# Centring the first chunk only, rotating it tile by tile out of PSUM, and loading late what is needed late

## The reference, cut to what matters

```python
x = x + attn(_layernorm(x), ...)      # no gamma, no beta
x = x + ffn(_layernorm(x), ...)
# in attn:
q = (x @ Wq.T).reshape(B, S, H, hd).transpose(0, 2, 1, 3)   # k, v alike
q = layernorm(q, q_gamma, q_beta)     # over the 8 entries of a head, eps 1e-5
q = q * cos + rotate_half(q) * sin    # k alike
scores = scale * jnp.einsum('bhqd,bhkd->bhqk', q, k)        # causal, softmax, times v, @ Wo.T + bo
```

## Time and profile before

| | us |
|---|---|
| median of 3 runs (lowest, highest) | 383.33 (382.54, 387.38) |
| the profiled execution, its own time | 383.55 |
| its span, first to last instruction | 381.7 |
| PE busy | 338.2 (89%) |
| DVE busy | 291.7 (76%) |
| ACT busy | 233.5 (61%) |
| POOL busy | 181.1 (47%) |

### The profile page before, as it was taken

One profiled execution on the slowest core, in us unless ns is written; L12 is line 12 of the kernel. 1 busy time (PEld: TensorE's weight loads), 2 busy tenths in 40 slices (PEclk: granted clock), 3 DMA queues, 4 the chain that ended last, 5 costly groups with the idle time before them and its releaser, 6 DMA issues.

```text
span 381.7 us, 7937 instructions
## 1 busy us (share of the span) xinstructions
PE 338.2 (89%) x2883; PEld 148.3 (39%) x2883; DVE 291.7 (76%) x508; ACT 233.5 (61%) x340; POOL 181.1 (47%) x304
## 2 busy tenths in 40 slices
PE   2667689899799898999999989999999999969995
PEld 1233345445444334353334332434334433434342
DVE  5693789899999999779998899987686830656742
ACT  1656129776759566774576767786676999424320
POOL 1587985998855438657504502034060028471000
PEclk9966559999999999999999999999999999988999
DMA  4997004103200036002043130001000019000000
GB/s 124 200 217 162 16 3 127 43 3 92 78 3 4 0 106 149 2 0 72 0 100 87 38 75 2 3 1 30 2 2 2 3 53 202 0 0 0 3 27 27
DMA packets 26840, 19.65 MB, mean 51 GB/s; under 512 B 9713, under 2 KB 23570, under 8 KB 26738
## 3 DMA queue, kind: packets, MB, share of 16 engines
q1 hardware_dynamic: 25410, 18.09, 20.8%
q10 hardware_dynamic: 1392, 1.05, 1.2%
HBM read 11.56 MB, written 1.15 MB: 33 GB/s over the span
## 4 chain that ended last, share of the span: by engine, by line
PE 61%; DVE 24%; issue 5%; ACT 5%; DMA 2%; POOL 1%; ACTq 1%; SPq 1%; DVEq 0%; POOLq 0%
PE psum L766 14%; PE psum L718 13%; PE psum L782 7%; PE psum L695 7%; PE psum L672 7%; DVE mx_diag L1159 7%; PE psum L644 5%; DVE mx_full L1159 4%; ACT probs L842 2%; PE psum L626 2%; DVE mv L1249 2%; PE psum L635 1%; PE psum L736 1%; PE psum L728 1%; DVE resid L1148 1%
## 5 line engine op out<-in xcount | busy, mean ns | idle before, releaser
L842 ACT ACTIVATE probs<-psum 128x1024 f32<-128x1024 f32 x144 | 142.3, 1024 | 49.7 <-PE psum L644 27.1
L1159 DVE TENSOR_REDUCE mx_diag<-psum 128x4 f32<-128x512 f32 (+2 forms) x96 | 96.0, 1041 | 23.3 <-PE psum L672 22.6
L1159 DVE TENSOR_REDUCE mx_full<-psum 128x2 f32<-128x1024 f32 x64 | 76.1, 1220 | 7.3 <-PE psum L672 7.0
L718 PE MATMUL psum<-probs,v_ones 128*18 128x512 f32 (+3 forms) x768 | 73.6, 489 | 0.2
L766 PE MATMUL psum<-x2T,w 128*128 128x512 f32 x144 | 71.8, 626 | 1.0 <-DVE mv L1249 0.9
L672 PE MATMUL psum<-k_st,q_st 62*128 62x512 bf16 (+3 forms) x384 | 60.6, 344 | 2.0 <-ACT probs L842 0.9
L644 PE MATMUL psum<-masks 64*128 64x128 bf16 (+2 forms) x896 | 51.5, 216 | 11.0 <-DVE mx_diag L1159 3.3
L695 PE MATMUL psum<-q_st,k_st 64*128 64x512 bf16 (+3 forms) x384 | 53.7, 328 | 3.1 <-DVE mv L1249 0.9
L644 PEld LDWEIGHTS psum<-masks 64*128 64x128 bf16 x896 | 33.6, 96 | 42.8 <-DVE mx_diag L1159 14.9
L1077 POOL TENSOR_SCALAR mh<-mh 128x512 f32<-128x512 f32 x27 | 16.8, 623 | 62.3 <-ACT mh L895 62.1
L1084 POOL TENSOR_TENSOR mh<-mh,mv 128x512 f32<-128x512 f32 x27 | 34.1, 1270 | 11.8 <-DVE mv L1249 11.8
(11 more groups left out here) (162 smaller groups left out, 359.0 us busy)
## 6 DMA issues: line engine op xcount, KB each, us to landing
early<-combine_scratch SPq DMA_DIRECT2D x24, 256.0 KB, 4.8
q_st<-parts SPq DMA_DIRECT2D x24, 128.0 KB, 2.4
k_st<-parts SPq DMA_DIRECT2D x18, 128.0 KB, 2.4
w<-in_We SPq DMA_DIRECT2D x3, 512.0 KB
k_st<-in_c_pad SPq DMA_DIRECT2D x8, 128.0 KB, 6.3
out<-xs SPq DMA_DIRECT2D x4, 256.0 KB, 2.3
xs<-in_x SPq DMA_DIRECT2D x3, 256.0 KB, 5.9
k_st<-parts ACTq DMA_DIRECT2D x6, 128.0 KB, 4.0
```

The source lines that it names most:

```text
L718: last = pe.matmul(acc[32 * j:32 * j + 2 * VC, q0:q0 + cols], own_then_zeros, probs[:, n % P_RING, j % 2, col:col + cols], start=(kt == 0 ...
L842: act.activation(probs[:, n % P_RING, :, :], wpair("scores", (s, i)), ACT.Exp, scale=SCALE).then_inc(exp_done, 1)
L1159: dve.tensor_reduce(dst[:, a % 2, :, pairs[0]:pairs[0] + nm, qt], w, AX.X, ALU.max, negate=True).then_inc(max_free, 1)
```

## The change

- For chunk 0, `norm` is now `centre` on DVE: a sum over the features and one operation that subtracts the mean. `stats` (means, variances and the factor on the heads' epsilon, `eps_x`) follows behind it, and POOL works out the deviation (`norm_rstd.0`) for v alone.
- Chunk 0's `qkv` becomes four `qk` products of 256 columns and one stage `vx` with the four v products. ACT only squares q and k (`square`) and copies v with the scale (`v_read`).
- `rotate` on DVE, once for each tile, multiplies q and k by cosine and sine straight from PSUM, adds the two products and sums the squares. The heads' deviation comes after that and is multiplied in by `scaled_and_shifted`, first for q (`rope_q`, which alone releases `qT.0`), then for k (`rope`).
- The rotary table and the four small vectors are issued by ACT behind x instead of by SP.
- `rest_loads` (8 pads of the stacks, Wo, the router's weights, bo) become the stage `late.0`, in SP's queue behind chunk 0's stacks; `expert_loads` (15 DMAs) become `late.1`, between `mrow.2` and `mrow.3`.
- The whole of `ORDER` is another sequence. Of what the prediction speaks of: ACT has `norm_apply.1` and `v_read.0` between `square.2` and `square.3`; on POOL `norm_rstd.2` now stands between `kT_low.0` and `rstd_pool.1`, and `tables_pool.0` between `kT_low.1` and `mneg.3`; chunk 2's `norm_apply`, `xT` and `qkv` come behind the first maxima. Behind the last attention product (`pv.79`) PE had six expert products ahead of `proj.3` and has three.

```diff
-NORM_ON_DVE = (("norm", 0), ("norm2", NX - 1))
+NORM_ON_DVE = (("norm2", NX - 1),)
+weights.0@0 ones.0 ones.1 norm.0 stats.0 weights_read.0 tables.0 xT.0@4 xT_read.0 qk.0@3 qk.1@6 square.0 norm.1 square.1
+vx.0@4 qk.2@5 square.2 norm_rstd.0 norm_rstd.1 norm_apply.1 rotate.0 v_read.0 rotate.1 qk.3@1 square.3 xT.1@6 xT_read.1
+qkv.4@4 qkv.5@2 qkv.6@0 rotate.2 rotate.3 qkv_read.4 qkv_read.5 qkv_read.6 qkv.7@2 qkv_read.7 headrstd.0 rope_q.0 rope.0
+qT.0@6 qT_lead.0 qT_rest.0 qT_mid.0 norm.2 qT_low.0 stack.0.0.0 kT.0@2 kT_lead.0 kT_rest.0 stack_act.0.1.0 norm.3
...
-            sp.dma_start(rope[:, :, :, :], c_rope).then_inc(ld_rope, 16)
-            for n, v in enumerate((q_gamma, q_beta, k_gamma, k_beta)):
-                sp.dma_start(gb[:, n, :], v.partition_broadcast(P)).then_inc(ld_rope, 16)
+                if kind == "late":
+                    (rest_loads, expert_loads)[arg]()
...
+            def first_qk(t):
+                w = fill("qk", t)
+                pe.wait_ge(work_read_act, frees("act", max(FILL["weights", 0], FILL["xT", 0]) + 1))
+                pe.matmul(w[:, 0:2 * P], xnT[:, t * P:(t + 1) * P], w_qkv[:, 0:2 * P], start=True, stop=True
+                          ).then_inc(work_full, 1)
+
+            def first_v():
+                w = fill("vx", 0)
+                pe.wait_ge(work_read_act, frees("act", max(FILL["weights", 0], FILL["xT", 0]) + 1))
+                for t in range(TPC):
+                    last = pe.matmul(w[:, t * P:(t + 1) * P], xnT[:, t * P:(t + 1) * P], w_qkv[:, 2 * P:3 * P],
+                                     start=True, stop=True)
+                last.then_inc(work_full, 1)
...
+            act.dma_start(rope[:, :, :, :], c_rope).then_inc(ld_rope, 16)
+            for n, v in enumerate((q_gamma, q_beta, k_gamma, k_beta)):
+                act.dma_start(gb[:, n, :], v.partition_broadcast(P)).then_inc(ld_rope, 16)
...
+            def first_squares(t):
+                act.wait_ge(work_full, turned("qk", t))
+                both = wbank("qk", t)[:, 0:2 * P].rearrange("p (n d m) -> p n d m", n=4, d=HD)
+                act.activation(sq[0][:, t, :, :, :, :].rearrange("p w r m d -> p (w r) d m"), both, ACT.Square
+                               ).then_inc(squared, 1)
+
+            def first_values():
+                act.wait_ge(work_full, turned("vx", 0))
+                act.wait_ge(norm_ready, 1)
+                act.wait_ge(v_set, 1)
+                for t in range(TPC):
+                    last = act.activation(v_ones[:, 0, t, 0:H, 1, 0:HD],
+                                          wbank("vx", 0)[:, t * P:(t + 1) * P].rearrange("p (h d) -> p h d", h=H),
+                                          ACT.Identity, scale=rstd[:, 0, 0, t:t + 1])
+                last.then_inc(work_read_act, 1)
...
+                    if step == 2 and kind == "norm" and x == 0:
+                        last.then_inc(norm_ready, 1)
+                        return
...
+            def centre():
+                link(dve.tensor_reduce(sums_x[:, :], xs[:, 0, :, :], AX.X, ALU.add))
+                dve.scalar_tensor_tensor(out=xn[0], in0=sums_x[:, :].unsqueeze(2).broadcast_to([P, TPC, P]), scalar=-1.0 / P,
+                                         in1=xs[:, 0, :, :], op0=ALU.mult, op1=ALU.add).then_inc(xn_ready, 1)
+
+            def first_stats():
+                for t in range(TPC):
+                    last = dve.bn_stats(stats[:, 0, 0, t, :], xs[:, 0, t, :])
+                link(last)
+                for t in range(TPC):
+                    last = dve.bn_aggr(mean_var[:, 0, 0, t, :], stats[:, 0, 0, t, :])
+                link(last)
+                dve.tensor_scalar(eps_x[:, :], mean_var[:, 0, 0, :, 1], EPS, EPS, ALU.add, ALU.mult).then_inc(norm_stats, 1)
+
+            def rotate(t):
+                dve.wait_ge(squared, t + 1)
+                z = wbank("qk", t)[:, 0:2 * P]
+                by_head = z.rearrange("p (n d m) -> p n d m", n=4, d=HD)
+                cos = g_cos[:, 0, t, :, :, :].rearrange("p w k d -> p (w k d)").unsqueeze(2).broadcast_to([P, 4 * HD, H // 2])
+                sin = g_sin[:, 0, t, :, :, :].rearrange("p w k d -> p (w k) d")
+                own = qk[0][:, t, :, :, :, :].rearrange("p w k d m -> p (w k d) m")
+                other = roped[:, t, :, :, :, :].rearrange("p w k d m -> p (w k) d m")
+                dve.tensor_tensor(own, z.rearrange("p (n m) -> p n m", m=H // 2), cos, ALU.mult)
+                for j in range(2):
+                    last = dve.tensor_tensor(other[:, :, 4 * j:4 * j + 4, :], by_head[:, :, 1 - j::2, :],
+                                             sin[:, :, 4 * j:4 * j + 4].unsqueeze(3).broadcast_to([P, 4, 4, H // 2]), ALU.mult)
+                link(last)
+                dve.tensor_tensor(own, own, roped[:, t, :, :, :, :].rearrange("p w k d m -> p (w k d) m"), ALU.add)
+                dve.tensor_reduce(ssum[:, 0, 2 * H * t:2 * H * (t + 1)], sq[0][:, t, :, :, :, :].rearrange("p w k m d -> p (w k m) d"),
+                                  AX.X, ALU.add).then_inc(work_read_dve, 1)
+
+            def scaled_and_shifted(w):
+                z = qk[0][:, :, w, :, :, :]
+                by_head = hrstd[:, :].rearrange("p (t w k m) -> p t w k m", t=TPC, w=2, k=2)[:, :, w, :, :]
+                for k in range(2):
+                    last = dve.tensor_tensor(z[:, :, k, :, :], z[:, :, k, :, :],
+                                             by_head[:, :, k, :].unsqueeze(2).broadcast_to([P, TPC, HD, H // 2]), ALU.mult)
+                link(last)
+                added = g_add[:, 0, :, w, :, :].rearrange("p t k d -> p t (k d)").unsqueeze(3).broadcast_to([P, TPC, 2 * HD, H // 2])
+                return dve.tensor_tensor(roped[:, :, w, :, :, :].rearrange("p t k d m -> p t (k d) m"),
+                                         z.rearrange("p t k d m -> p t (k d) m"), added, ALU.add)
...
+                sums = ssum[:, 0, :].rearrange("p (t n) -> p t n", t=TPC)
+                link(dve.scalar_tensor_tensor(out=sums, in0=sums, scalar=1.0 / HD, in1=eps_x[:, :].unsqueeze(2).broadcast_to(
+                    [P, TPC, 2 * H]), op0=ALU.mult, op1=ALU.add))
```

## The result

The changed kernel takes 392.73 us (median of 4 runs, 391.83 to 394.89), the kernel before 383.94 on the same chips: a ratio of 1.0281, interval 1.0223 to 1.0338. Forecast were 381.0 us and a range of 375.5 to 386.5; the result lies above it. The profiled execution took 394.89 us, with a span of 393.1.

The account below looks back on a forecast made before the run. The prediction took PE, busy 89% of the span, as the fullest engine, idle mainly in the first 60 us. Gains of 1.1 + 1.5 - 0.5 + 0 + 0, plus 0.4 for the clock, gave 383.55 - 2.5 = 381.05 us, range 375.5 to 386.5.

Parts of the forecast that it names:

- Step 1: Prologue up to the rotation: centring readies xnT near 8.2 us, first square at 9.8; gain so far 2.4 us.
- Step 2: Chunk 0's rotation on DVE: 1.5 us per tile, three through at 15.2; the fourth, behind norm_apply.1, ends at 21.5.
- Step 3: From the heads' sums to the first maxima: hrstd at 25.0, first maxima at 37.5 (36 to 39), 2.5 us gained.
- Step 4: Chunk 1's stacks and maxima: stacks land at 68.1 instead of 69.2, gaining 1.1 us, plus 1.5 of earlier PE work.
- The rival of the half clock: Chunk 2's transposes and products among first maxima at half clock: up to 3 us lost, 384 to 385; chance 0.07.
- Step 5: Late expert loads on SP ahead of mrow.3: scores.9 waits nothing to 5 us, taken as half a microsecond.
- Step 6: Middle and end: reordered stages worth minus 4 to plus 4 us, value 0; fewer expert products before proj.3, value 0.
- The sum: Whole kernel: 1.1 + 1.5 - 0.5 + 0 + 0 = 2.1, plus 0.4 for an earlier full clock: 2.5 us faster.
- The tell-tales: Signs of failure: scores.9 waiting microseconds for a DMA, middle waits changing by over 4, first maxima at 40 again.

Follow-up runs that it names:

- e3: Changed kernel with the rotary table and four gamma/beta loads back on SP behind the centring matrix: 392.91 us, ratio 1.0252 to the kernel before.
- e8: Changed kernel with routing stages apart, pads after chunk 0's stacks land, expert loads in five groups of three: 393.43 us, ratio 1.0249 to the kernel before.
- e7: New arithmetic, order of the kernel before from the first maxima on, loads up front, chunk 2's products between first maxima: 385.84 us, ratio 1.0074 to the kernel before.
- e16: Like the hybrid of new arithmetic and old order, loads up front, but chunk 2's products ahead of the first maxima: 381.50 us, ratio 0.9960 to the kernel before.
- e17: Kernel before with only the 15 expert loads late, in one block behind mrow.2: 390.30 us, ratio 1.0214 to the kernel before.
- e2: Changed kernel with both groups of late loads before SP's first stack: 389.91 us, ratio 1.0172 to the kernel before.
- e15: Kernel before with chunk 0's routing stages 2 and 3 directly behind stage 1 on DVE: 387.97 us, ratio 1.0163 to the kernel before.
- e11: New arithmetic, old order, chunk 2's products ahead of first maxima, pads after chunk 0's stacks, expert loads in pieces: 382.27 us, ratio 1.0010 to the kernel before.
- e14: New arithmetic, old order, chunk 2's products before first maxima, late loads in pieces, mturn.0 later, centring loads and square.3 first: 379.10 us, ratio 0.9920 to the kernel before.
- e4: Kernel before with both load groups late: pads behind mneg.0, expert loads behind mrow.2: 390.41 us, ratio 1.0203 to the kernel before.

## Why the prediction was wrong

- **Step 1** failed in one sentence: "The loads that move to ACT's queue cost nothing". ACT's issues are free, their data aren't: issued beside x and the weights they hold back the matrix, which lands at 7.85 and, with them back on SP behind it, at 5.23 (e3). Given the early matrix, the working holds: e3's `xnT` is done at 8.13 (forecast 8.2) and its first square starts at 9.45 (9.8).
- **Step 2** was right in mechanism and size: `rotate` takes 1.6 us (1.5), `square.3` ran behind `norm_apply.1` at 19.09, the fourth rotation ended at 21.35 (21.5). The third one ended at 17.76 and not at 15.2, by the error of step 1; the end came out right because POOL's second chain sets it, as forecast, and that chain doesn't need the matrix.
- **Step 3** holds to the issues: `hrstd` at 24.95 (25.0), q at 26.5 and k at 27.9 (26.5, 28.0), ACT's last DMA at 33.54 (33.8). The term behind is mis-sized: that DMA took 5.82 us, not 2.4 to 3.7, and the first maxima came at 40.25 instead of 37.5, outside my ends of 36 to 39. About 1.5 us of it are the pads (e8), which is what I had let them count for, so the rest of the miss, 2.8 us on DVE, is there without them (e8: 38.76 where the sum had 36). That the stacks' own transfers make it up is likely and not shown.
- **Step 4** failed: chunk 1's maxima came at 72.22 instead of 68.1. POOL's rotation ended at 58.2 (57), and "4 us of that were slack" didn't hold: `qT.1` came at 60.16, 3.3 us behind the earlier trace rows. Two things then arrive together. Chunk 0's 24 reductions ended near 71.7 instead of 68.7, with chunk 2's products and `pv.1`, `pv.2` between them. And the stacks landed at 72.2: the low parts were done at 65.6, near the forecast 64.7, but SP's twelve issues, begun at 61.47, take 0.6 us each, and the last started at 69.71, not at 65.6. The sum had no term for that queue. The `pv` products I counted among "1.5 us of PE work done earlier", a gain; chunk 2's products stood in it only as 0.4 us gained by an earlier full clock, and e7 against e16 shows them as a loss of 3 to 4 us. The rival of the half clock had this mechanism, at up to 3 us and a chance of 0.07.
- **Step 5** failed in what it took. I had the bounds (7 to 13.2 us of issues, 0 to 5 us of stall) and the waiting stage right, and took about 8.5 us of issues and half a microsecond, because "the queues are nearly empty there". The issues took 12.8 us and the stall was 1.83; the DMA engines were 0.76 busy meanwhile, with the block's own data among them. The shared experts' weights, 64 KB each, take 1.9 us to issue where the large ones take 0.4. The nearest row was the 13.2 us, the only measurement there was. e17 prices the block at 2.1% in the kernel before, e2 both groups at 1.1% here.
- **Step 6** failed as much: "value 0" for an order of 1326 stages. The new order costs about 4 us (e7 against e2), at the end of my bounds. One cause is shown in the old order, the row of routing (e15); it was in the list that I read. I compared counts of stages ahead of chosen marks and never asked how long DVE does nothing that PE waits for.
- **The sum** was minus 2.5; it should have been about plus 10, as the chain of runs adds up: 1.1% for the loads (changed kernel to e2), 1.0% for the order (e2 to e7), 1.1% for chunk 2's products (e7 to e16), less the 0.4% that e16 leaves for the prologue, an interval that holds zero. Each link is uncertain by 0.5 to 0.8 of a per cent.
- **The tell-tales** that I named did show it: `scores.9` waiting 1.83 us for a DMA, waits in the middle changed by 5, first maxima at 40 again.

## What to carry to other kernels

A load taken out of the prologue isn't free where it goes: count its issue time on the queue, name the first small DMA behind it and who waits for that, and split the block or put it where the queue is idle. In a hand-written order, look for the longest row of one engine's work that the bounding engine doesn't need; moving the stage that shows the wait only hands the wait on. Before speeding up what comes first, find what sets the next hand-over: here chunk 1's rotation on POOL, so that 2.75 us (e11) and 4.1 us (e14) won at the first maxima were worth 0.6 and 0.3 us at 69 us.

## What the runs showed of the hardware

- DVE's operations on 128x64 elements with two SBUF inputs take 0.22 us as a rule, and 1.57 and 2.39 us in the routing of the changed kernel, while POOL made operations of 1.97 and 2.35 us on 128x1024; each of the two ends 0.08 us behind the POOL operation beside it. The two make the row of routing 3.5 us longer. That isn't new, though: the kernel before has five such operations in its routing, 3.3 us in all, but not in one row. The Trainium skill (SBUF — State Buffer, Who interferes with whom) has DVE and GpSimd lock their shared port for a whole instruction; the trace agrees, with an eleven-fold time here.
- In `late.1` of the changed kernel an issue on SP takes 0.40 to 0.44 us for most loads, of 8 to 512 KB, and 0.8 to 1.9 us for the shared experts' weights of 64 KB; it isn't the size that counts. The first of these weights took 3.44 us in the prologue of the kernel before and 4.83 in e2, where the DMA engines were full.
- After PE's quiet stretches the clock is at its lower level of 1.2 GHz just when the held-up work starts: 0.50 in 120 to 124 us of e15, behind 1.26 us of work in the 4 us before, and 0.57 in 88 to 96 us of e4, behind 0.52 us of work in 84 to 88. Waits of 4.8 and 5.45 us went with 1.6% and 2.0% of the time, 6 to 8 us.
